# A hybrid vision network on one core: the depthwise stages' tile transfers, rings and share of blocks on TensorE

## The chip, the core and the metric

The program runs on one core of a Trainium2 chip. The core has TensorE (PE, matrix products into PSUM), VectorE (DVE), ScalarE (ACT), GpSimd (POOL) and SyncE (SP, which here issues nearly all DMAs), and sixteen DMA engines that move data between HBM and the on-chip memory (SBUF). Each engine runs its own instructions in order and waits on semaphores for the others. A wait on SP therefore holds up every transfer behind it. The metric is the device time of one execution in microseconds.

## The reference

The network takes 32 images of 96 channels and 32 x 32 pixels, float32, through four layers. What matters here is the second half of layer 0, an MLP over four volumes of eight frames, with a depthwise 3 x 3 x 3 convolution before each of its two channel products:

```python
def dsconv3d(x, dw_w, dw_b, pw_w, pw_b):
    y = jax.lax.conv_general_dilated(x, dw_w, (1, 1, 1), [(1, 1)] * 3,
                                     dimension_numbers=('NCDHW', 'OIDHW', 'NCDHW'), feature_group_count=x.shape[1])
    y = jax.nn.gelu(y + dw_b[None, :, None, None, None], approximate=False)
    y = jnp.einsum('bcdhw,oc->bodhw', y, pw_w) + pw_b[None, :, None, None, None]
    return y

def mlp(x, t, h, w, p):
    ...
    xg = dsconv3d(xg, p['dw1_w'], p['dw1_b'], p['pw1_w'], p['pw1_b'])   # 96 channels, then 96 -> 384
    xg = dsconv3d(xg, p['dw2_w'], p['dw2_b'], p['pw2_w'], p['pw2_b'])   # 384 channels, then 384 -> 96
```

So dw1 convolves 96 channels and dw2 384, each over 4 volumes x 8 frames of 1024 pixels, with 27 taps for each channel, zero beyond the edges, and a bias and GELU behind. The rest of the network (selective scans, convolutions, Fourier mixing, a quantised feed-forward) is untouched by the change.

## The kernel before

The kernel is one program of stages, each a function with its own SBUF and PSUM tensors; a stage begins when the one before has ended. `build` calls `volume_conv` for dw1 (line 2986), `l0_expand` (the product 96 to 384, stage `pw`), `volume_conv` for dw2 (line 2989), then `l1_in_proj`. In the profile both depthwise stages carry the tile prefix `dw_`.

`volume_conv` (line 936) takes the channels in blocks of 32. Of each three blocks two go through TensorE and one through taps, side by side. Three blocks are a *step*; a block on TensorE is a *unit*. dw1 has 1 step (2 units), dw2 has 4 steps (8 units).

**TensorE's way.** A tile holds 4 frames x 32 channels on 128 partitions and 1024 pixels, 512 KB. SP loads it (`load_raw`, line 1014; two buffers), DVE transposes it in 32 x 32 squares (`turn_in`, line 1216) into `xin`, where a partition is a frame and a column x, and the free dimensions are channel and row y. Eight tiles fill a unit. For each of the 32 channels PE multiplies banded matrices (`wb`, three rows of taps) and small edge matrices for the frames next to the group of four (`we`): 3 whole and 6 edge products in the code, each run as two matmuls in the trace. Weights for two channels (a pair) come by three DMAs (`load_weights`, line 1020) into four slots; a slot is loaded again when PE is done with the pair four before. ACT adds the bias, applies GELU and writes into `stg` (`evacuate`, line 1131); PSUM holds 8 channels. When a unit's 32 channels are there, DVE transposes its eight tiles back (`turn_back`, line 1225) into `ot` (three buffers), and SP stores them (`store_tile`, line 1035). `stg` holds one unit, so ACT's first evacuation of a unit waits for all eight back transposes of the unit before (line 1134).

**The taps' way.** For the third block a partition is a volume and a channel. The eight frames lie in `vol`, one buffer each (`load_frame`, line 1029). For each frame DVE does 15 taps (10 for the first and last frame) by multiply-and-add in PSUM (`pd`), ACT opens `acc` with one tap and makes 11 products (7) that POOL adds into `acc`; DVE merges both sums into `sm`, ACT adds bias and GELU in `close`, SP stores (`store_frame`, line 1041).

**Order.** Each engine's order is written out by hand. DVE runs all eight back transposes of a unit in one go at the start of the next (line 1248), and one transpose in after each six taps (line 1271). ACT spreads evacuations among its products by a count of operations (`catch_up`, line 1170), none before the ninth. SP's list goes by unit and pair j (line 1061): weights three pairs ahead, two tile stores at each j below 4, raw loads and frames at fixed j. The first loads of a stage are lines 1046 to 1060.

A tile moves by one DMA whose DRAM side has the shape (4, 32, 1024), 4 frames or 4 volumes by 32 channels.

Of the kernel before, what the change touches and what calls it, by code (L numbers as in the profile page):

```python
# [935 lines left out]
def volume_conv(nc, stage, src, dst, band, edge, bias, taps_w, steps, func):  # L936

    T = 8
    PAIRS, SLOTS = 16, 4
    PRODS, RAWS, OUTS = 4, 2, 3  # L940
    UNITS = 2 * steps
# [36 lines left out]
    def block_of(u):  # L978
        return 3 * (u // 2) + u % 2

    def four_frames(of, u, t):
# [4 lines left out]
    def all_volumes(of, i, f):  # L986
        block = 3 * i + 2
        return of.rearrange("(v f) c n -> f v c n", f=FRAMES)[f, :, 32 * block:32 * block + 32, :]

    with ExitStack() as stack:  # L990
        r = Room(nc, stage, stack)
        xin = r.sb("xin", [128, 2, 32, T, SIDE])
        stg = r.sb("stg", [128, 32, T, SIDE])
        raw = r.sb("raw", [128, RAWS, HW]); ot = r.sb("ot", [128, OUTS, HW])
        wb = r.sb("wb", [128, SLOTS, 2, 3, 128]); we = r.sb("we", [128, SLOTS, 2, 2, 3, 32])
        vol = r.sb("vol", [128, FRAMES, HW])
# [4 lines left out]
        s_raw = [r.dma_sem(f"raw{k}") for k in range(RAWS)]  # L1001
        s_band = [r.dma_sem(f"band{k}") for k in range(SLOTS)]
        s_vol = [r.dma_sem(f"vol{f}") for f in range(FRAMES)]
# [6 lines left out]

        with nc.Block() as block:
            @block.sync
            def _(sp):
                def load_raw(q):
                    if q < T * UNITS:
                        if q >= RAWS:
                            sp.wait_ge(turned, nth(q - RAWS))
                        sp.dma_start(raw[:, q % RAWS, :], four_frames(src, q // T, q % T)).then_inc(s_raw[q % RAWS], 16)

                def load_weights(q):  # L1020
                    if q < PAIRS * UNITS:
                        k = q % SLOTS
                        if q >= SLOTS:
                            sp.wait_ge(mm, nth(2 * (q - SLOTS) + 1))
                        sp.dma_start(wb[:, k, :, :, :], band[q]).then_inc(s_band[k], 16)
                        sp.dma_start(we[0:32, k, 0, :, :, :], edge[q, 0]).then_inc(s_band[k], 16)
                        sp.dma_start(we[96:128, k, 1, :, :, :], edge[q, 1]).then_inc(s_band[k], 16)

                def load_frame(i, f):
                    if i < steps:  # L1030
                        if i > 0:
                            sp.wait_ge(merged, nth((i - 1) * FRAMES + min(f + 1, FRAMES - 1)))
                        sp.dma_start(vol[:, f, :], all_volumes(src, i, f)).then_inc(s_vol[f], 16)

                def store_tile(u, t):
                    if u >= 0:
                        q = T * u + t
                        sp.wait_ge(back, nth(q))
                        sp.dma_start(four_frames(dst, u, t), ot[:, q % OUTS, :]).then_inc(s_ot[q % OUTS], 16)

                def store_frame(i, f):
                    if i >= 0:
                        sp.wait_ge(done, nth(i * FRAMES + f))
                        sp.dma_start(all_volumes(dst, i, f), sm[:, f % 2, :]).then_inc(s_sm[f % 2], 16)
# [6 lines left out]
                for f in range(3):  # L1051
                    load_frame(0, f)
                    load_raw(2 + 2 * f)
                    load_raw(3 + 2 * f)
                load_weights(1)
                load_weights(2)
                for f in range(3, FRAMES):
                    load_frame(0, f)
                load_raw(8)
                load_raw(9)  # L1060
                for u in range(UNITS):
                    i, s = u // 2, u % 2
                    for j in range(PAIRS):
                        load_weights(PAIRS * u + j + 3)
                        if j < 4:
                            store_tile(u - 1, 2 * j)
                            store_tile(u - 1, 2 * j + 1)
                        if j == 4 and s == 0:
                            load_frame(i, 5) if i else None
                            load_frame(i, 6) if i else None  # L1070
                            load_frame(i, 7) if i else None
                        if j == 4 and s == 1:
                            load_frame(i + 1, 1)
                            load_frame(i + 1, 2)
                        if j in (4, 6, 8, 9, 11, 13, 14, 15):
                            load_raw(T * (u + 1) + (4, 6, 8, 9, 11, 13, 14, 15).index(j) + RAWS)
                        if j == 5:
                            store_frame(i if s else i - 1, 2 if s else 6)
                            store_frame(i if s else i - 1, 3 if s else 7)
                        if j == 10 and s == 0:  # L1080
                            load_frame(i + 1, 0)
                        if j == 10 and s == 1:
                            load_frame(i + 1, 3)
                            load_frame(i + 1, 4)
                        if j == 13:
                            store_frame(i, 4 * s)
                            store_frame(i, 4 * s + 1)
# [2073 lines left out]
```

## Time and profile before

| | us |
|---|---|
| median of 3 runs | 19247.6 (19228.68 to 19251.41) |
| profiled execution | 19248.37 |
| its span | 19246.6, mean TensorE clock 0.947 |
| PE, DVE, ACT, POOL busy over the span | 88%, 85%, 80%, 67% |
| first transfer of dw1 to first of `pw` | 6046.46 to 6400.70 |
| first transfer of dw2 to first of the next stage | 6598.58 to 7820.44 |

The page gives busy time for the whole span; the two depthwise stages are 8% of it, so their limits show only in stretches cut out of it. PE's clock is shown as a share of its full speed; the two levels are 1.2 and 2.4 GHz, 0.50 and 1.00. In timelines the instructions of one kind that follow each other are merged: "x6" and the length of all six. The DMA share is the mean busy share of the sixteen DMA engines.

### The profile page before, as it was taken

Reading aid. Unit: us, or ns where it says so; the run is one execution under the profiler, and the core shown is the slowest. Engines: PE = TensorE matmul, PEld = TensorE weight load, DVE = VectorE, ACT = ScalarE, POOL = GpSimd, SP = SyncE. Lnnn points to the kernel's source line nnn. Section 1 sums busy time; section 2 is a strip of 40 time slices with the busy share of each in tenths; the row PEclk is TensorE's granted clock in tenths of the full one; section 3 lists DMA queues with packets and bytes.
Section 4 is the critical chain, followed back from the end, with each engine's and each line's share of the span. In section 5 each row is a group of like instructions: output and inputs, shape, how many; then the busy total and the mean of one; then the engine's idle time right before and its main releaser. Section 6 shows DMA issues by size and latency. Waiting matters only on the chain. (4 is left out here: it accounts for less than half of the span.)

```text
span 19246.6 us, 270014 instructions
## 1 busy us (share of the span) xinstructions
PE 16951.7 (88%) x77576; PEld 10108.8 (53%) x77576; DVE 16299.4 (85%) x12434; ACT 15364.9 (80%) x24406; POOL 12882.4 (67%) x6390
## 2 busy tenths in 40 slices
PE   8799997899985565798899999999999999989798
PEld 3455553555542244344466666666666666547374
DVE  4799998899975276378899999999999999979798
ACT  7699996899962444476699999999999999835556
POOL 0199991799952265154499999999999999800101
PEclk9899998999987787899999999999999999999899
DMA  5788876787886543656633333333333333352313
GB/s 176 233 241 242 247 242 211 236 243 236 251 228 187 194 139 135 223 214 257 266 112 111 111 112 117 112 111 118 116 111 112 117 112 111 111 160 57 103 52 98
DMA packets 857608, 3157.91 MB, mean 164 GB/s; under 512 B 106166, under 2 KB 139674, under 8 KB 831644
## 3 DMA queue, kind: packets, MB, share of 16 engines
q1 hardware_dynamic: 842396, 3091.03, 50.0%
q10 hardware_dynamic: 13824, 50.34, 0.7%
q8 instruction: 631, 10.34, 0.2%
q14 instruction: 757, 6.20, 0.1%
HBM read 2335.65 MB, written 805.32 MB: 163 GB/s over the span
## 5 line engine op out<-in xcount | busy, mean ns | idle before, releaser
L1929 DVE TENSOR_TENSOR_SCAN l1s_h<-l1s_da,l1s_pd 128x1024 f32<-128x1024 f32 x3072 | 6783.1, 2268 | 236.9 <-PE l1s_pd L1861 161.4
L1972 ACT ACTIVATE l1s_dm<-l1s_dut,l1s_bt 128x384 f32<-128x384 f32 x7424 | 4061.7, 605 | 74.8 <-PE l1s_pd L1861 74.6
L1955 ACT ACTIVATE l1s_da<-l1s_dl,l1s_a 128x1024 f32<-128x1024 f32 x3072 | 3502.0, 1140 | 30.7 <-DVE l1s_h L1929 29.6
L1861 PE MATMUL l1s_pd<-l1s_id,l1s_dm 128*128 128x128 f32 x22272 | 2973.0, 275 | 36.3 <-DVE l1s_h L1929 33.9
L1861 PEld LDWEIGHTS l1s_pd<-l1s_id,l1s_dm 128*128 128x128 f32 x22272 | 2562.1, 142 | 492.0 <-issue 288.2
L1835 POOL TENSOR_TENSOR l1s_pb<-l1s_h,l1s_cc 128x1024 f32<-128x1024 f32 x1024 | 2519.5, 2460 | 86.1 <-DVE l1s_h L1929 75.6
L1839 POOL TENSOR_TENSOR l1s_pa<-l1s_sm,l1s_cc 128x1024 f32<-128x1024 f32 x1024 | 2435.2, 2378 | 0.0
L1872 PE MATMUL l1s_py<-l1s_pb,l1s_both 128*128 128x512 f32 x4096 | 2157.2, 608 | 193.7 <-POOL l1s_pb L1835 193.5
L1830 POOL TENSOR_TENSOR l1s_sm<-l1s_h 128x1024 f32<-128x1024 f32 x928 | 2204.7, 2376 | 130.2 <-DVE l1s_h L1929 130.1
L1872 PE MATMUL l1s_py<-l1s_pa,l1s_id 128*128 128x512 f32 x4096 | 2114.4, 598 | 0.3 <-POOL l1s_pa L1839 0.3
L2795 POOL TENSOR_TENSOR l0sf_pr<-l0sf_h,l0sf_cc 128x1024 f32<-128x1024 f32 x768 | 1811.5, 2375 | 67.5 <-DVE l0sf_h L2877 52.7
L2795 POOL TENSOR_TENSOR l0sb_pr<-l0sb_h,l0sb_cc 128x1024 f32<-128x1024 f32 x768 | 1812.6, 2377 | 61.7 <-DVE l0sb_h L2877 57.5
L2540 POOL CAST ffn_h<-ffn_z 128x1024 fp8e5<-128x1024 f16 x128 | 180.9, 1414 | 2260.1 <-DVE ffn_z L2560 2237.6
L1855 PEld LDWEIGHTS l1s_pd<-l1s_bd,l1s_dut 128*128 128x128 f32 x4608 | 832.6, 191 | 1463.7 <-issue 825.5
L2833 PE MATMUL l0sf_py<-l0sf_pr,l0sf_id 128*128 128x512 f32 x3072 | 1580.0, 597 | 0.0
L2833 PE MATMUL l0sb_py<-l0sb_pr,l0sb_id 128*128 128x512 f32 x3072 | 1578.9, 596 | 0.0
L2925 ACT ACTIVATE l0sb_dm<-l0sb_dut,l0sb_bt 128x192 f32<-128x192 f32 x3584 | 1316.4, 447 | 9.2 <-DMA l0sb_dl<-l0dlsb 9.2
L2925 ACT ACTIVATE l0sf_dm<-l0sf_dut,l0sf_bt 128x192 f32<-128x192 f32 x3584 | 1313.6, 443 | 9.6 <-DMA l0sf_dl<-l0dlsf 9.6
L1210 POOL TENSOR_TENSOR dw_acc<-dw_acc,dw_prod 128x961 f32<-128x961 f32 (+2 forms) x400 | 897.0, 2288 | 552.8 <-ACT dw_prod L1158 550.3
L2813 PEld LDWEIGHTS l0sf_pd<-l0sf_id,l0sf_dm 128*128 128x128 f32 x6144 | 762.4, 142 | 928.1 <-issue 683.8
L2813 PEld LDWEIGHTS l0sb_pd<-l0sb_id,l0sb_dm 128*128 128x128 f32 x6144 | 761.9, 142 | 922.9 <-issue 680.8
L1112 PE MATMUL dw_pc<-dw_xin,dw_wb 128*128 128x248 f32 (+1 forms) x1920 | 572.2, 433 | 615.7 <-DMA dw_we<-in_dw_edge 222.6
(310 smaller groups left out, 31634.3 us busy)
## 6 DMA issues: line engine op xcount, KB each, us to landing
l1s_cc<-crows SPq DMA_DIRECT2D x1024, 512.0 KB, 3.7
l0sf_cc<-l0crowsf SPq DMA_DIRECT2D x512, 512.0 KB, 5.4
l0sb_cc<-l0crowsb SPq DMA_DIRECT2D x512, 512.0 KB, 5.4
l0sf_cc<-l0crowsf SPq DMA_DIRECT2D x512, 256.0 KB, 7.1
l0sb_cc<-l0crowsb SPq DMA_DIRECT2D x512, 256.0 KB, 7.0
dls<-l1p_dl SPq DMA_DIRECT2D x192, 512.0 KB, 6.9
duts<-l1p_dut SPq DMA_DIRECT2D x64, 1536.0 KB, 5.9
l1s_dut<-duts SPq DMA_DIRECT2D x64, 1536.0 KB, 7.2
```

The source lines that it names most:

```text
L1830: pool.tensor_tensor(sm[:, rnd % 2, :], h[:, rnd * HT % 4, :], h[:, (rnd * HT + 1) % 4, :], ALU.add)\
L1835: pool.tensor_tensor(pb[:, rnd % 2, :], h[:, (rnd * HT + 2) % 4, :], cc[:, rnd % 4, :], ALU.mult)\
L1839: pool.tensor_tensor(pa[:, rnd % 2, :], sm[:, rnd % 2, :], cc[:, rnd % 4, :], ALU.mult)\
L1861: mm = pe.transpose(pd[:, s % 2, blk * 128:blk * 128 + 128], dm[:, rnd % 2, blk, j * 128:j * 128 + 128], idt[:, :])
L1872: mm = pe.matmul(target[:, hs], weights[:, :], row[:, hs], start=(rnd == 0), stop=(rnd == ROUNDS - 1))
L1929: dve.tensor_tensor_scan(h[:, s % 4, :], da[:, j, :], pd[:, s % 2, :], 0.0, ALU.mult, ALU.add)\
L1955: act.activation(da[:, j, :], dl[:, half, j, :], ACT.Exp, scale=a[:, HT * half + j, n:n + 1])\
L1972: ins = act.activation(dm[:, rnd % 2, blk, :], dut[:, half, blk, :], ACT.Identity, scale=bt[:, half, blk, n:n + 1])
L2795: pool.tensor_tensor(pr[:, s % 4, :], h[:, s % 6, :], cc[:, rnd % 4, j, :], ALU.mult).then_inc(prod, 1)
L2813: mm = pe.transpose(pd[:, half, at:at + 128], dm[:, rnd % 2, blk, COLUMNS[j]:COLUMNS[j] + 128], idt[:, :])
L2833: mm = pe.matmul(py[:, j, HALVES[half]], idt[:, :], pr[:, s % 4, HALVES[half]], start=(n == 0), stop=(n == N - 1))
L2925: ins = act.activation(out, src, ACT.Identity, scale=b)
```

## The change

- `volume_conv` takes `per_step`, the blocks on TensorE per step. dw1 keeps 2 (of 3). dw2 gets 3 of 4: 3 steps, 9 units and 3 tap blocks in place of 4 steps, 8 units and 4 tap blocks.
- Each tile and each frame moves by four DMAs of 32 rows (128 KB) in place of one. Semaphores count 64 a tile.
- One more tap of the six inner frames goes from DVE to ACT and POOL (12 products in place of 11).
- `stg` becomes a ring of 48 channels in three halves of 16. The middle unit of three starts with its second 16 channels (`in_order`). ACT waits for back transposes two units old before its first half and one unit old before its second.
- `vol` becomes a ring of 6 frames, weights have 3 slots (from 4), products 3 (from 4), `ot` 2 buffers (from 3). At the start of a stage tiles 2 to 5 land in `ot` and `sm`.
- DVE's transposes in and back are placed among the taps by their share of the unit. ACT's evacuations are spread over the step, with no minimum of nine. SP's order is by slice of a step.
- The tables on the host are laid out for the new blocks.

```diff
-    PAIRS, SLOTS = 16, 4
-    PRODS, RAWS, OUTS = 4, 2, 3
-    UNITS = 2 * steps
+    PAIRS, SLOTS = 16, 3
+    PRODS, RAWS, OUTS, RING = 3, 2, 2, 6
+    UNITS = per_step * steps
...
-        share = 11 if len(depths) == 3 else 7
+        share = 12 if len(depths) == 3 else 7
...
+    def four_frames(u, t):
 
         first = t % SEQS * FRAMES + t // SEQS * 4
-        return of[first:first + 4, 32 * block_of(u):32 * block_of(u) + 32, :]
+        rows = channels((per_step + 1) * (u // per_step) + u % per_step)
+        return [(slice(32 * j, 32 * j + 32), first + j, rows) for j in range(4)]
...
+    def in_order(u, n):
+        return (n + 16) % 32 if u % 3 == 1 else n
...
                 def load_raw(q):
                     if q < T * UNITS:
-                        if q >= RAWS:
-                            sp.wait_ge(turned, nth(q - RAWS))
-                        sp.dma_start(raw[:, q % RAWS, :], four_frames(src, q // T, q % T)).then_inc(s_raw[q % RAWS], 16)
+                        to, sem, _ = landing(q)
+                        if q >= 6:
+                            sp.wait_ge(turned, nth(q - 6 if q < 8 else q - RAWS))
+                        for rows, image, of in four_frames(q // T, q % T):
+                            sp.dma_start(to[rows, :], src[image, of, :]).then_inc(sem, 16)
...
                 load_raw(0)
                 load_raw(1)
                 load_all(sp, s_w, consts)
+                for f in range(3):
+                    load_frame(0, f)
+                for q in range(2, 6):
+                    load_raw(q)
                 sp.wait_ge(zeroed, nth(0))
                 load_weights(0)
...
                 load_weights(1)
+                load_raw(6)
+                load_raw(7)
+                for f in range(3, RING):
                     load_frame(0, f)
                 load_raw(8)
...
+                for i in range(steps):
+                    for j in range(SLICES):
+                        u, w = per_step * i + j // PAIRS, j % PAIRS
+                        load_weights(PAIRS * u + w + 2)
+                        if w % 2 == 0:
+                            load_raw(T * (u + 1) + w // 2 + 1)
+                        if 2 <= w < 10:
+                            store_tile(u - 1, w - 2)
+                        if j == at(0.04) and i:
+                            load_frame(i, 3)
+                            load_frame(i, 4)
+                            load_frame(i, 5)
+                        if j == at(0.15):
+                            store_frame(i - 1, 6)
+                            store_frame(i - 1, 7)
+                        if j == at(0.27):
+                            load_frame(i, 6)
+                        if j == at(0.40):
+                            store_frame(i, 0)
+                            store_frame(i, 1)
...
-                    if c == 0 and u:
+                    if n == 0 and u > 1:
+                        act.wait_ge(back, nth(T * (u - 1) - 1))
+                    if n == 16 and u:
                         act.wait_ge(back, nth(T * u - 1))
                     act.wait_ge(mm, nth(q | 1))
...
-                        while out < 32 and max(9, (out // 2 + 1) * steps_here // 16 + 1) <= passed:
-                            evacuate(u, out)
+                        while out < CHANNELS * (i + 1) and (out % CHANNELS // 2 + 1) * WHOLE // (CHANNELS // 2) + 1 <= passed:
+                            evacuate(out)
...
+                        share = (n + 1) * per_step / TAPS + per_step * i
+                        while outs < T * UNITS and share >= outs // T + 1 + 0.06 + 0.06 * (outs % T):
+                            turn_back(outs)
+                            outs += 1
+                        while share >= ins // T - 1 + (ins % T + 1) / T and ins < T * UNITS:
+                            turn_in(ins)
+                            ins += 1
...
-                w["dw2_band"], w["dw2_edge"], w["dw2_bias"], w["dw2_taps"], 4, ACT.Gelu)
+                w["dw2_band"], w["dw2_edge"], w["dw2_bias"], w["dw2_taps"], 3, 3, ACT.Gelu)
```

## Rows read from the trace of the kernel before

**Rows 1.** Stretches: length; busy (count) PE, PEld, DVE, ACT, POOL; clock; DMA share; GB/s

```profile
6046.46:6400.70 354.24, 153.82 (x1152) 109.65 (x1152) 196.10 (x150) 127.30 (x161) 180.68 (x81) 0.71 0.33 112
6598.58:7820.44 1221.86, 669.92 (x4608) 458.33 (x4608) 782.26 (x600) 496.33 (x640) 719.04 (x321) 0.76 0.38 130
6598.58:6663.87 65.29, 0.00 (x0) 0.00 (x0) 15.16 (x9) 9.53 (x9) 11.35 (x6) 0.50 0.32 113
6925.29:7502.00 576.71, 341.89 (x2303) 230.94 (x2302) 390.84 (x301) 246.66 (x320) 359.30 (x161) 0.79 0.40 137
7759.89:7820.44 60.55, 0.00 (x0) 0.00 (x0) 14.95 (x9) 1.26 (x2) 0.00 (x0) 0.50 0.22 87
6066.50:6095.50 29.00, 0.00 (x0) 0.00 (x0) 7.61 (x4) 1.15 (x1) 0.00 (x0) 0.50 0.26 105
6162.00:6198.00 36.00, 36.00 (x291) 26.36 (x291) 29.50 (x24) 27.73 (x36) 35.69 (x17) 1.00 0.55 159
6410.00:6580.00 170.00, 165.01 (x358) 61.12 (x357) 0.00 (x0) 98.53 (x90) 0.00 (x0) 0.99 0.96 337
```

**Rows 2.** Timeline, dw1's lead-in, DVE: start, length, instruction, [idle before <- releaser]

```profile
6056.54 1.90 DVE L1222 STREAM_TRANSPOSE dw_xin<-dw_raw 128x1024 f32<-128x1024 f32 x1 [16.27 <-DMA dw_raw<-n]
6061.54 1.90 DVE L1222 STREAM_TRANSPOSE dw_xin<-dw_raw 128x1024 f32<-128x1024 f32 x1 [3.09 <-DMA dw_raw<-n]
```

**Rows 3.** Waits in dw2: us in total, times, longest

```profile
DVE dw_xin L1222 <- DMA dw_raw<-hid: 432.1, 27, 232.5
...
ACT dw_stg L1136 <- DVE dw_ot L1232: 289.9, 7, 44.1
...
DVE dw_ot L1232 <- DMA g<-dw_ot: 191.0, 40, 11.5
```

**Rows 4.** Timeline, SP's DMA issues in dw1

```profile
6133.06 1.05 SPq L1026 DMA_DIRECT2D dw_we<-in_dw_edge  x1
...
6157.98 0.35 SPq L1025 DMA_DIRECT2D dw_wb<-in_dw_band  x1
6158.37 0.43 SPq L1026 DMA_DIRECT2D dw_we<-in_dw_edge  x1
6158.84 0.42 SPq L1027 DMA_DIRECT2D dw_we<-in_dw_edge  x1
...
6162.44 0.35 SPq L1025 DMA_DIRECT2D dw_wb<-in_dw_band  x1
```

**Rows 5.** DMA issues between dw1 and dw2: count, KB each, median us to landing

```profile
hid<-pw_out ACTq DMA_DIRECT2D x96, 512.0 KB, 3.9
...
pw_wt<-in_pw SPq DMA_DIRECT2D x1, 144.0 KB, 2.1
```

**Rows 6.** Timeline, PE in dw1, DVE and POOL in dw2

```profile
6150.80 1.22 PE L1112 MATMUL dw_pc<-dw_xin,dw_wb 128*128 128x256 f32 x2 [24.19 <-DMA dw_we<-in_dw_edge]
...
6744.75 6.93 DVE L1262 SCALAR_TENSOR_TENSOR dw_pd<-dw_vol,dw_wt,dw_pd 128x992 f32<-128x992 f32 x6
6751.60 1.99 DVE L1222 STREAM_TRANSPOSE dw_xin<-dw_raw 128x1024 f32<-128x1024 f32 x1
...
6712.96 81.11 POOL L1210 TENSOR_TENSOR dw_acc<-dw_acc,dw_prod 128x992 f32<-128x992 f32 x36 [24.69 <-ACT dw_prod L1158]
```

**Rows 7.** Groups of dw2 by form: busy us, mean ns, idle before

```profile
L1158 ACT ACTIVATE dw_prod<-dw_vol,dw_wt 128x961 f32<-128x961 f32 x176 | 188.1, 1100 | 48.3 <-POOL dw_acc L1210 48.1
...
L1222 DVE STREAM_TRANSPOSE dw_xin<-dw_raw 128x1024 f32<-128x1024 f32 x64 | 125.8, 1965 | 432.1 <-DMA dw_raw<-hid 432.1
L1232 DVE STREAM_TRANSPOSE dw_ot<-dw_stg 128x1024 f32<-128x1024 f32 x64 | 120.9, 1908 | 191.0 <-DMA g<-dw_ot 191.0
...
L1136 ACT ACTIVATE dw_stg<-dw_pc,dw_bt 128x256 f32<-128x256 f32 x256 | 106.7, 476 | 525.4 <-DVE dw_ot L1232 289.9 <-PE dw_pc L1112 235.4
...
L1240 DVE TENSOR_TENSOR dw_sm<-dw_pd,dw_acc 128x1024 f32<-128x1024 f32 x32 | 37.6, 1214 | 11.1 <-POOL dw_acc L1210 10.1 <-issue 0.9
```

More of the change, by code:

```diff
@@ L1001, in volume_conv @@
         s_raw = [r.dma_sem(f"raw{k}") for k in range(RAWS)]
+        s_lead = [r.dma_sem(f"lead{k}") for k in range(4)]
         s_band = [r.dma_sem(f"band{k}") for k in range(SLOTS)]
-        s_vol = [r.dma_sem(f"vol{f}") for f in range(FRAMES)]
+        s_vol = [r.dma_sem(f"vol{k}") for k in range(RING)]
         s_ot = [r.dma_sem(f"ot{k}") for k in range(OUTS)]
@@ L1058, in _ @@
+                load_raw(7)
+                for f in range(3, RING):
                     load_frame(0, f)
                 load_raw(8)
[L1060 to L1072, printed above, removed]
+                SLICES = PAIRS * per_step
@@ L1082, in _ @@
[L1082 to L1087, printed above, removed]
+                        if j == at(0.92):
+                            store_frame(i, 4)
+                            store_frame(i, 5)
                 for t in range(T):
@@ L1092, in _ @@
                 for k in range(OUTS):
-                    sp.wait_ge(s_ot[k], 16 * len(range(k, T * UNITS, OUTS)))
+                    sp.wait_ge(s_ot[k], 64 * T * UNITS // OUTS)
                 for k in range(2):
-                    sp.wait_ge(s_sm[k], 16 * steps * FRAMES // 2)
+                    sp.wait_ge(s_sm[k], 64 * steps * FRAMES // 2)
             @block.tensor
@@ L1270, in _ @@
                             merge(i, f + 1)
-                        if (n - start) % 6 == 5 and turned_in < T:
-                            turn_in(u + 1, turned_in)
-                            turned_in += 1
-                for t in range(T):
-                    turn_back(UNITS - 1, t)
+                        share = (n + 1) * per_step / TAPS + per_step * i
[5 more added lines that the diff above has]
+                            ins += 1
+                while outs < T * UNITS:
+                    turn_back(outs)
+                    outs += 1
 def l0_expand(nc, g1, w, hid):
@@ L3085, in volume_tables @@
                 rows[z][:, :, :, to + x - 1, to] = cubes[:, :, z, :, x, None]
-        rows = rows.transpose(0, 1, 2, 4, 3, 5).reshape(3, steps * 16 * 2, 2, 32, 3, 32).swapaxes(2, 3)
-        band = np.zeros((steps * 32, 4, 32, 2, 3, 4, 32), f)
+        pairs = steps * per_step * 16
+        rows = rows.transpose(0, 1, 2, 4, 3, 5).reshape(3, pairs, 2, 32, 3, 32).swapaxes(2, 3)
+        band = np.zeros((pairs, 4, 32, 2, 3, 4, 32), f)
         for to in range(4):
@@ L3090, in volume_tables @@
                 band[:, of, :, :, :, to] = rows[of - to + 1]
-        flat = blocks[:, 2].repeat(4, axis=0).reshape(steps, 4, 32, 27).reshape(steps, 128, 27)
-        parts = offsets.reshape(steps, 3, 32)
-        last = parts[:, 2].repeat(4, axis=0).reshape(steps, 128, 1)
-        return {"band": band.reshape(steps * 32, 128, 2, 3, 128), "edge": np.stack([rows[2], rows[0]], 1),
-                "bias": np.broadcast_to(parts[:, :2].reshape(1, steps * 2, 32), (128, steps * 2, 32)),
-                "taps": cat([flat, last], 2).swapaxes(0, 1)}
-    for name in ("dw1", "dw2"):
-        for part, table in volume_tables(v[f"L0_conv_{name}_w"], v[f"L0_conv_{name}_b"]).items():
+        parts = offsets.reshape(steps, per_step + 1, 32)
+        last = cat([blocks[:, per_step], parts[:, per_step, :, None]], 2)
+        bias = parts[:, :per_step].reshape(1, steps * per_step, 32)
+        return {"band": band.reshape(pairs, 128, 2, 3, 128), "edge": np.stack([rows[2], rows[0]], 1),
+                "bias": np.broadcast_to(bias, (128, steps * per_step, 32)),
+                "taps": last[:, None].repeat(4, axis=1).reshape(steps, 128, 28).swapaxes(0, 1)}
+    for name, per_step in (("dw1", 2), ("dw2", 3)):
+        for part, table in volume_tables(v[f"L0_conv_{name}_w"], v[f"L0_conv_{name}_b"], per_step).items():
             w[f"{name}_{part}"] = table
```

183 lines of the change are left out of this document (98 added, 85 removed).

## The prediction

> **What bounds the kernel now.** I read the page first: its 40 slices show one stretch, near a third of the span, where every engine is partly idle, and its groups place the depthwise program there. A chain of waits for the last instruction is of no use here, since that ends in another stage. So I cut the span by the first transfer of each stage [rows 1]: dw1 lasts 354.2 us and dw2 1221.9 us, of which 65.3 us pass before its first tap and 60.6 us after its last merge. In the two middle steps (576.7 us, 288.4 us each) PE is busy 59%, DVE 68%, ACT 43%, POOL 62%, and the 16 DMA engines 40% at 137 GB/s. No engine is the bound.
>
> The transfers are. Two tiles of 512 KB, issued together, release their transposes at 6056.54 and 6061.54 [rows 2]: 5.0 us a tile. In a stretch that moves only such tiles the DMA share is 0.26 at 105 GB/s, while the stage between dw1 and dw2 moves 337 GB/s at 0.96 [rows 1]. So a tile transfer runs at the pace of about four engines of sixteen. A step of dw2 moves 48 tiles (16 loads and 16 stores of transposed tiles, 8 and 8 frames): 48 x 5.0 = 240 us. Its 32 pairs of weights (432 KB a pair, over all engines) take of each engine a sixteenth of 432 KB, at 512/4 KB in 5.0 us: 1.05 us, 34 us a step. Together 274 of 288 us: the four engines are full. The waits agree: transposes back wait 191 us for stores, transposes in 432 us for loads (232.5 us of it between the stages) [rows 3].
>
> The Trainium skill says why, in "DMA: Bandwidth & Descriptors", section "Why a DMA increments its semaphore by 16 and not by 1": a transfer is spread over the largest number up to 16 that divides the slowest dimension of both sides. A source of (4, 32, 1024) gets 4, and the trace agrees (0.26 of 16 is 4.2). For 32 rows it gives 16. No row of before shows a 128 KB transfer of 32 rows, so the new width stays a bet, which I carry as a rival.
>
> **Part 1, four DMAs of 32 rows.** I take it that they use all engines: the transfers of the stage that reaches 0.96 have 96 or 128 rows in a single dimension, the tiles have 4 by 32, and the pieces again a single one. So the 5.0 us go; one 512 KB piece of work then takes 512 KB / 337 GB/s = 1.6 us [rows 1]. What is late next is SP, which issues them. Back-to-back issues start 0.47 us apart, the 32-row edge loads among them [rows 4]; behind full queues the same instruction took 1.05 us [rows 4]. A tile costs SP 4 x 0.47 = 1.88 us, a pair of weights 3 issues, 1.3 us. A new step of dw2 has 48 x 3 + 48 x 4 + 16 x 4 = 400 issues, 188 us (before: 144). Bytes: 64 tiles and 48 pairs are 54 MB, in 250 us 217 GB/s, below 337.
>
> The lead-in: SP issues two tiles, 2 constants, three frames, four tiles, 6 weight pieces and two tiles, 52 issues; the last starts after 51 x 0.47 = 24.0 us, lands some 2.3 us later, and its transpose of 1.9 us [rows 7] ends at 28.4 us with 0.2 us to wake DVE. The landing is my choice between 2.1 us for 144 KB and 3.9 us for 512 KB at full load [rows 5]. Against 65.3 us this saves 37 us in each stage.
>
> The tail: with two buffers each store (1.88 us and landing) holds the next transpose but one, 5.6 us for two. Eight end 20.6 us after the merge, then one tile and two frames are issued (5.6 us) and land: 28 us, and 2 to 3 us to the next stage. Before: 60.6 us.
>
> **Part 2, three of four blocks on TensorE in dw2.** Nine units instead of eight, three steps of taps instead of four. PE at full clock takes 4.46 us for two channels, seen in the distance of the weight issues that wait for it [rows 4], with PE busy 36.00 of 36.00 us at clock 1.00 [rows 1]: 71.4 us a unit. DVE has 104 taps a step (110 less the one tap moved for each of six inner frames), at 1.14 us from start to start, and 48 transposes at 1.85 us [rows 6], and 8 merges [rows 7] at 1.14 us: 118.6 + 88.8 + 9.1 = 216.5 us, 72.2 us a unit. POOL has 86 adds at 81.11/36 = 2.25 us [rows 6]: 194 us. ACT has 96 evacuations of 0.48 us and 86 products and 16 whole frames of 1.1 us each [rows 7]: 158 us. PE and DVE are level, and POOL is hidden under both in dw2.
>
> **Part 3, the order on SP and two buffers.** This is where I put a new wait. In slice w of a unit (one slice per channel pair) SP loads weights; in even slices it then waits for a transpose in and issues a raw tile; in slices 2 to 9 it then stores a tile back. DVE's back transpose t+2 waits until store t has landed, because OUTS is 2. So from one transpose in to the next, over two slices: raw 1.88 us, store 3 x 0.47 us to its last piece, landing 2.3 us; then on DVE back, two taps, back, transpose in, 8.0 us. Sum 13.6 us, against 8.9 us that PE needs for two slices. The loop turns three times: the first transpose in ends at 5 taps and three transposes, 11.3 us, the fourth at 52.1 us; the rest of the unit is 16.7 taps, four transposes and its merges, 29.4 us. A unit lasts 81.5 us instead of 72. Behind SP in this loop stand the weights, so PE stalls too. After a wait PE's first pair is slow: started at 6150.80 [rows 6], done by 6157.98 [rows 4], 7.2 us instead of 4.46. I add 3 us a unit for one such pair and for the 64 frame issues a step: 84.5 us. Bounds of a unit: 72.5 us if landing and order hide everything, 91 us with landing 3.9 us and issue 0.56 us.
>
> The end of a step is a loop of its own: last product, add, merges, transpose in, PE's next unit, some 5.7 us, twice. The first unit has no backs (71.4 + 2.7), the last no loads (76).
>
> The longer stage queue costs nothing in bandwidth; SLOTS 3 instead of 4 gives weights two pairs, 8.9 us, for 1.3 us of issue and the landing, enough unless SP is late, which is in the 3 us. PRODS 3 instead of 4: POOL ran 36 adds without a gap with ACT at 1.1 us beside its 2.25 us, so nothing. The ring of six frames: frame 7 waits for merge 2 and is read a quarter of a step later; nothing. The ring of 48 channels takes away ACT's wait for all eight back transposes (289.9 us) [rows 3]; PE's stalls behind it go with that.
>
> **Sum, dw2:** 28.4 + 74.1 + 7 x 84.5 + 76 + 2 x 5.7 + merges and tail 35 = 816 us, against 1221.9: 406 us saved.
>
> **dw1** has one step, two units, no raw loads in the second, so the loop does not turn: stores come at PE's pace. POOL bounds it. ACT now evacuates the first pair before its fourth product, so POOL's fourth add starts when PE's first pair is done: 28.4 + 7.2 + 1.9 = 37.5 us. Then 83 adds x 2.25 = 187 us, 5 us where ACT waits for unit 1 to begin, merges 2.3, tail 28, 2 us over: 262 us, against 354.2: 92 us saved.
>
> The profiled execution took 19248.4 us, its span 19246.6, the median of runs 19247.6, so they may be used for one another. 19248 - 406 - 92 = 18750 us. Under 0.2% of the total (39 us) a measurement can't tell a change from none.
>
> **Rivals.**
> (a) The loop is hidden; the stage runs at PE's and DVE's 73 us a unit: 28 + 74 + 8 x 73 + 11 + 35 = 733 us. 18,667 us. For it: DVE's waits for stores come in a bunch today and are spread by the change. Against it: two buffers, and SP in order. 0.16.
> (b) SP is dearer than 0.47 us an issue, for the queues are partly filled: at 0.8 us a step needs 320 us of SP, a unit 107 us, dw2 970 us, dw1 20 us more: 18,920 us. For it: 1.05 us in a burst [rows 4]. Against it: those bursts stood behind four-engine tiles, which go. 0.13.
> (c) The change doesn't do what it says: 32-row pieces move at 105 GB/s too. dw2 moves 3 x 64 tiles, the same 192 as before: 3 x (320 + 50) + 95 = 1205 us, dw1 as before. 19,230 us. 0.04.
> (d) Slower: each issue holds SP's queue for longer than 0.94 us on average. dw2 has 1200 issues, and 1200 x 0.94 + 95 us is the 1222 us of today; that is the point from which it decides. At 1.1 us: 1415 us, and dw1 near 354: 19,440 us. Such an issue (1.05 us) is in the trace only behind full queues; in the steady row it is 0.47. 0.04.
>
> The Trainium skill, in "DMA: Bandwidth & Descriptors", speaks for (d) in the section "Anatomy of one DMA — SWDGE (gpsimd) path": a fixed 2.0 us beside bytes at 436 GB/s. By its figures a 128 KB piece is 2.3 us, four in series 9.2 us, 192 tiles 1770 us. The trace contradicts the series: 96 stores and 32 loads of a mean 480 KB keep 337 GB/s with 3.9 us to landing each [rows 1, 5], so transfers overlap and the fixed part is a delay.
>
> **Chances.** Forecast 0.63, between 18,700 and 18,850 on its own bounds. The low end of the range is (a), 18,665; the high end 18,850 is the loop at 91 us a unit with slower tails (7 x 6.5 = 46 us, and as much again for SP's lateness). Faster by over 0.2%: forecast, (a), (b) and a part of the rest, 0.94; within 0.2%: most of (c), 0.03; slower 0.03.
>
> **What would show it.** DMA share against GB/s in dw1's first 30 us: 279 GB/s or so instead of 105 at 0.26. dw2's stage length 816 us, first PE matmul 28 us after the first issue. DVE's back transposes waiting for stores in the middle units, some 12 us a unit; if they wait for nothing, (a). The issues on SP 0.47 us apart; if more, (b) or (d). In dw1 POOL without gaps after 38 us. I am wrong in mechanism if units of 84 us come with DVE waiting for evacuations or merges and not for stores.

## The result, and the profile after

The kernel after takes 18782.0 us (median of 4 runs, 18774.3 to 18805.6), the kernel before 19238.1 us in the same comparison: ratio 0.9769, 95% interval 0.9755 to 0.9782. Forecast: 18750 us, range 18665 to 18850.

The stretches of the profiled execution after: dw1, dw2, its lead-in, its middle step, its tail. The columns are those of [rows 1]:

```profile
6031.70:6297.20 265.50, 153.26 (x1152) 109.05 (x1152) 189.22 (x144) 135.12 (x167) 193.94 (x87) 0.78 0.55 149
6495.40:7359.30 863.90, 694.26 (x5184) 491.98 (x5184) 654.84 (x480) 428.58 (x594) 582.42 (x259) 0.90 0.68 192
6495.40:6527.26 31.86, 0.01 (x1) 0.01 (x1) 15.30 (x9) 3.31 (x3) 3.37 (x2) 0.50 1.00 241
6786.40:7068.50 282.10, 233.45 (x1728) 164.74 (x1728) 217.96 (x161) 144.25 (x200) 196.17 (x87) 0.92 0.69 196
7325.10:7359.30 34.20, 0.00 (x0) 0.00 (x0) 17.00 (x10) 2.28 (x2) 0.00 (x0) 0.54 0.55 154
```

dw1 takes 265.5 us (before 354.2), dw2 863.9 us (before 1221.9): 446.7 us less. The two executions differ by 20 us more outside these stages, in code that the change leaves alone. The start of dw1 alone lies between 6019 and 6047 us in the thirteen profiled executions of this study, so lengths of stages are compared below, and totals only to about 20 us. Stages whose code is the same repeat closely: dw1 took 265.5 and 264.7 us (after, two_of_three), 234.0 and 233.0 (pool_start_dw1, late_evacuations), 233.5 and 232.9 (both_orders, late_and_order).

The middle step of dw2 (282.1 us, the fourth row) carries 196 GB/s at a DMA share of 0.69, where [rows 1] had 137 at 0.40. PE is busy 83% of it, DVE 77%, POOL 70%. Who waits in dw2 (total, times, longest):

```profile
ACT dw_stg L1177 <- PE dw_pc L1151: 305.0, 121, 22.7
POOL dw_acc L1252 <- ACT dw_prod L1200: 244.9, 54, 22.2
...
DVE dw_ot L1275 <- DMA g<-dw_ot: 120.6, 28, 10.4
...
PE dw_pc L1151 <- DMA dw_we<-in_dw_edge: 92.1, 27, 8.7
ACT dw_stg L1177 <- DVE dw_ot L1275: 77.3, 8, 13.6
...
DVE dw_sm L1284 <- POOL dw_acc L1252: 35.7, 4, 10.9
```

Against [rows 3]: DVE's wait for stores went from 191.0 to 120.6 us, though a store now lands 2.8 us after its issue (columns: count, KB each, median us from issue to landing, in the middle step):

```profile
dw_wb<-in_dw_band SPq DMA_DIRECT2D x48, 384.0 KB, 3.3
dw_raw<-hid SPq DMA_DIRECT2D x96, 128.0 KB, 3.2
g<-dw_ot SPq DMA_DIRECT2D x96, 128.0 KB, 2.8
```

The wait predicted for two buffers is there in the form predicted. One turn of the loop in the middle step, DVE first, then SP:

```profile
6812.98 1.96 DVE L1265 STREAM_TRANSPOSE dw_xin<-dw_raw 128x1024 f32<-128x1024 f32 x1
6814.80 2.31 DVE L1304 SCALAR_TENSOR_TENSOR dw_pd<-dw_vol,dw_wt,dw_pd 128x961 f32<-128x961 f32 x2
6821.50 1.93 DVE L1275 STREAM_TRANSPOSE dw_ot<-dw_stg 128x1024 f32<-128x1024 f32 x1 [4.38 <-DMA g<-dw_ot]
6823.36 2.34 DVE L1304 SCALAR_TENSOR_TENSOR dw_pd<-dw_vol,dw_wt,dw_pd 128x961 f32<-128x961 f32 x2
6825.60 1.94 DVE L1275 STREAM_TRANSPOSE dw_ot<-dw_stg 128x1024 f32<-128x1024 f32 x1
6827.47 1.89 DVE L1265 STREAM_TRANSPOSE dw_xin<-dw_raw 128x1024 f32<-128x1024 f32 x1
```

```profile
6814.97 1.70 SPq L1041 DMA_DIRECT2D dw_raw<-hid  x4
6816.72 2.63 SPq L1067 DMA_DIRECT2D g<-dw_ot  x4
```

The transpose in ends at 6814.94, SP issues the raw tile at once, then the store; DVE's back transpose waits for this store and starts at 6821.50, 2.2 us after SP has issued its last piece; two taps, a back, the next transpose in. From in to in 14.5 us, where 13.6 was forecast. Part of the difference is the store's four issues, 2.63 us here instead of 1.88. This turn is among the shorter ones: the 21 turns of the seven units with both loads and stores take 13.6 to 20.7 us, 16.2 on average. In the middle step SP itself waits 44.0 us for transposes in and 32.9 us for PE.

### The profile page after: what moved, and what is told of

The parts are those of the page before. It is cut to its first block and busy times, and to the rows that moved or that the text cites. A ratio compares the mean times of both kernels' runs of the same rounds, so it can differ in the third digit from the quotient of the medians.

```text
span 18779.8 us, 271646 instructions
## 1 busy us (share of the span) xinstructions
PE 16964.4 (90%) x78152; PEld 10133.1 (54%) x78152; DVE 16165.3 (86%) x12308; ACT 15304.7 (81%) x24366; POOL 12759.8 (68%) x6334
## 5 line engine op out<-in xcount | busy, mean ns | idle before, releaser
L1902 PE MATMUL l1s_pd<-l1s_bd,l1s_dut 128*128 128x128 f32 x4608 | 946.3, 287 | 182.6 <-issue 71.2
L2918 DVE TENSOR_TENSOR_SCAN l0sf_h<-l0sf_da,l0sf_st,l0sf_pd 128x512 f32<-128x512 f32 x768 | 981.8, 1278 | 116.8 <-PE l0sf_pd L2860 41.3
```

Source lines behind the costliest of these rows:

```text
L1902: pe.matmul(pd[:, s % 2, LAST * 128:], dut[:, half, LAST, j * 128:j * 128 + 128], bd[:, DIAGONAL.index(n), :], start=True, stop=True)
```

## The experiments

Lengths in us from one profiled execution each; the time is the median of its runs, the ratio is to the kernel before with its 95% interval.

| kernel | dw1 | dw2 | time | ratio |
|---|---|---|---|---|
| before | 354.2 | 1221.9 | | |
| after | 265.5 | 863.9 | 18782.0 | 0.9769 (0.9755 to 0.9782) |
| one_dma_per_tile | 356.6 | 1363.3 | 19378.0 | 1.0077 (1.0057 to 1.0097) |
| before_four_dmas | 246.6 | 862.0 | 18751.3 | 0.9751 (0.9732 to 0.9771) |
| two_of_three | 264.7 | 950.9 | 18863.5 | 0.9810 (0.9790 to 0.9829) |
| three_out_buffers | 259.6 | 792.0 | 18715.4 | 0.9731 (0.9714 to 0.9747) |
| store_before_raw | 264.5 | 810.3 | 18735.3 | 0.9743 (0.9726 to 0.9759) |
| eight_pieces | 301.3 | 1082.7 | 19036.2 | 0.9901 (0.9881 to 0.9921) |
| one_weight_dma | 260.6 | 802.0 | 18724.3 | 0.9737 (0.9721 to 0.9754) |
| pool_start_dw1 | 234.0 | 792.4 | 18684.6 | 0.9721 (0.9705 to 0.9737) |
| late_evacuations | 233.0 | 775.6 | 18667.9 | 0.9708 (0.9691 to 0.9724) |
| both_orders | 233.5 | 775.6 | 18664.0 | 0.9709 (0.9693 to 0.9725) |
| late_and_order | 232.9 | 758.0 | 18636.1 | 0.9696 (0.9680 to 0.9713) |

**One DMA per tile again.** The one edit, at all four places where a tile or frame moves, with semaphore counts to match:

```diff
-                        for rows, image, of in four_frames(q // T, q % T):
-                            sp.dma_start(to[rows, :], src[image, of, :]).then_inc(sem, 16)
+                        sp.dma_start(to, whole_tile(src, q // T, q % T)).then_inc(sem, 16)
```

> The kernel after, with each tile and frame moved by one DMA of shape (4, 32, 1024) again, all else as after. Theory (tiles ran at the pace of four engines, and their width is what the change buys): a step of dw2 has 64 tiles at 5.0 us = 320 us and 48 pairs of weights at 1.05 us = 50 us on the same four engines, so three steps take 1110 us, and with lead-in 65 and tail 60 dw2 takes about 1200 to 1240 us, dw1 about 350 us; total 19200 or above, within 0.5% of the kernel before. Rival (the gain is in DVE's and ACT's new order and the block moved to TensorE): dw2 stays under 1000 us and the total under 18950.

```profile
6602.40:7965.70 1363.30, 772.66 (x5184) 528.70 (x5184) 656.32 (x480) 427.78 (x594) 581.69 (x259) 0.76 0.37 121
```

The whole gain is gone and dw2 is 141 us slower than before the change, 0.77% on the total. The theory stands, and its number is too low by over 120 us. The share of 0.37 is a mean over sixteen engines and hides that four of them are nearly full. By the packet records of this trace, the middle step (456.6 us) has 1446 us of 4096-byte packets, nearly all of them tiles, 362 on each of four engines, and 1218 us of weights and the rest, 76 on each of sixteen: some 438 of 457 us on the four. The forecast had 320 + 50 = 370. So a pair of weights costs each engine about 1.5 us and not the 1.05 us of the forecast and of the prediction, and a tile's packet takes 175 ns on average, where it took 159 ns in the stretch of [rows 1] with tiles alone. That tiles run on just four engines is the assumption in this estimate; the records don't name the engine.

**The kernel before with four DMAs.**

```diff
-                        sp.dma_start(raw[:, q % RAWS, :], four_frames(src, q // T, q % T)).then_inc(s_raw[q % RAWS], 16)
+                        for rows, image, of in four_frames(q // T, q % T):
+                            sp.dma_start(raw[rows, q % RAWS, :], src[image, of, :]).then_inc(s_raw[q % RAWS], 16)
```

> The kernel before with only the transfers changed: each tile and frame by four DMAs of 32 rows. Theory: the four-engine bound goes, and what is left is the order: all eight back transposes in one go, with ACT and PE waiting for them. DVE has 207 us a step of two units, and each unit adds some 15 us of waiting, so a unit takes 105 to 115 us against 144, dw2 about 930 to 990 us, dw1 about 275 us, total about 18880 to 18960. Rival (the order matters most and the transfers only fit it): dw2 over 1100 us. Rival (the transfers are everything): dw2 at 864 us or less, total at 18780.

```profile
6475.60:7337.60 862.00, 625.31 (x4608) 443.52 (x4608) 782.83 (x600) 502.85 (x640) 719.31 (x321) 0.83 0.64 184
```

```profile
ACT dw_prod L1164 <- POOL dw_acc L1216: 169.3, 188, 1.2
...
ACT dw_stg L1142 <- DVE dw_ot L1238: 115.8, 7, 17.7
...
DVE dw_ot L1238 <- DMA g<-dw_ot: 29.2, 21, 2.1
...
PE dw_pc L1118 <- DMA dw_we<-in_dw_edge: 12.5, 4, 4.1
```

The rival "the transfers are everything" holds: 862.0 us in dw2, and 246.6 in dw1, 19 us better than the whole change; the totals are too close for their intervals to tell apart. My theory had 930 to 990 us: I took 15 us of waiting a unit, with PE and ACT stopped behind the eight back transposes. The waits in the second fence are short, 115.8 us for ACT in seven units, 29.2 us for stores with three buffers, 12.5 us for weights, and yet a unit takes 102 us. The reason is DVE's own work. Four of the middle units (two steps):

```profile
6691.10:7099.90 408.80, 314.38 (x2304) 222.49 (x2304) 391.26 (x302) 251.26 (x321) 359.08 (x161) 0.85 0.67 193
```

DVE is busy 391.3 of 408.8 us, 96%, and PE 77%. With quick tiles the kernel before is bound by DVE, and moving a block from the taps to TensorE is what takes work off DVE. That only pays where nothing else holds a unit up, which the next runs show.

**Two of three blocks in dw2, within the kernel after.**

```diff
-                w["dw2_band"], w["dw2_edge"], w["dw2_bias"], w["dw2_taps"], 3, 3, ACT.Gelu)
+                w["dw2_band"], w["dw2_edge"], w["dw2_bias"], w["dw2_taps"], 4, 2, ACT.Gelu)
```

> The kernel after with dw2 at two of three blocks on TensorE and four steps, as before the change. Theory (the loop sets a unit's length): a unit has 52 taps, the loop ends at about 60 us, the rest is 42 us: 102 us a unit, 8 units, dw2 about 880 to 900 us; moving the third block to TensorE is worth 20 to 40 us only. Rival (POOL, 194 us a step, sets it): 97 us a unit, about 850 us. Rival (the split is a main part of the gain): dw2 over 950 us.

dw2 took 950.9 us, so the rival "a main part" is right at its edge and the theory 50 us short. With this kernel the change is taken apart, in dw2: transfers 1221.9 to 862.0 (-359.9); new order, rings, two out buffers in place of three and the one tap a frame 862.0 to 950.9 (+88.9); the third block on TensorE 950.9 to 863.9 (-87.0). The last two cancel. This holds for this order of the steps alone, and how the 88.9 us divide was not tried; three_out_buffers below takes 71.9 us off the kernel with the third block by the buffer alone. In dw1, which has no third block, the kernel after is 18.9 us behind before_four_dmas. The third buffer gives back 5.9 us of it (259.6). POOL's six more adds, 86 instead of 80 at 2.25 us, are 13.5 us by an estimate. So the order itself costs dw1 next to nothing.

**Three out buffers.**

```diff
-    PRODS, RAWS, OUTS, RING = 3, 2, 2, 6
+    PRODS, RAWS, OUTS, RING = 3, 2, 3, 6
```

> The kernel after with three buffers for tiles transposed back in place of two. Theory (loop of transpose in, raw issue, store issue, landing, back transpose): with three buffers a store gates the third back transpose behind it, the loop's 13.6 us for two slices fall to about 10.5 us, DVE's waits for stores (120.6 us in dw2) fall under 40 us, and a middle unit falls from 87 or more to 75 to 80 us: dw2 775 to 815 us, total 18700 to 18735. Rival (SP's 400 issues a step are the bound, by their number): dw2 stays within 15 us of 864, and waits move from stores to weights.

```profile
DVE dw_sm L1284 <- POOL dw_acc L1252: 42.8, 5, 13.2
ACT dw_stg L1177 <- DVE dw_ot L1275: 33.1, 8, 6.4
DVE dw_ot L1275 <- DMA g<-dw_ot: 32.4, 17, 4.5
```

72 us for 4 KB a partition. In the middle step SP's waits for transposes in fall from 44.0 to 17.6 us. Waits for stores fall to 32.4 us, ACT's for the ring from 77.3 to 33.1. Units 3 and 4 fall from 86.9 and 88.7 us (from the last transpose in of one unit to that of the next) to 76.2 and 78.9. Unit 5, the last of its step, falls only from 106.6 to 95.2.

**Store before raw load**, with two buffers:

```diff
-                        if w % 2 == 0:
-                            load_raw(T * (u + 1) + w // 2 + 1)
                         if 2 <= w < 10:
                             store_tile(u - 1, w - 2)
+                        if w % 2 == 0:
+                            load_raw(T * (u + 1) + w // 2 + 1)
```

> The kernel after (two out buffers) with two lines of SP's list exchanged: in each slice the store of a tile goes ahead of the raw load and of its wait for a transpose in. Same instructions, same number of issues. Theory (the loop through SP's wait is what lengthens a unit): the loop is then raw 1.88, weights 1.4, store 1.4 to its last piece, landing 2.3, back, transpose in, 10.7 us instead of 13.6 for two slices, three times in each of seven units: dw2 60 us shorter, 795 to 815 us, and DVE's waits for stores fall from 120 us to 40 to 70 us. Rival (only the number of buffers or of issues counts, not their order): dw2 within 15 us of 864.

```profile
DVE dw_ot L1275 <- DMA g<-dw_ot: 79.0, 30, 6.8
```

53.6 us less in dw2 from the place of one call, no instruction added or taken away. It is a second, independent cut through the loop, and waits fall less than forecast (79.0 us) but the stage as forecast. Number of issues alone is excluded as the cause.

**Eight pieces of 16 rows.**

```diff
-        return [(slice(32 * j, 32 * j + 32), first + j, rows) for j in range(4)]
+        return [(slice(16 * j, 16 * j + 16), first + j // 2, half(rows, j % 2)) for j in range(8)]
```

> The kernel after with each tile and frame by eight DMAs of 16 rows (64 KB) in place of four of 32. Bytes the same, the engines used the same by the theory of width. Theory (SP's issue time is close under the bound): 656 issues a step x 0.47 = 308 us, so three steps 925 us, lead-in about 45 us, tail about 50 us: dw2 1010 to 1060 us, dw1 290 to 310 us, total 18960 to 19030. Rival (issues are hidden, only landing and order count): dw2 under 900 us. Rival (a fixed cost of 2 us a transfer in series): over 1500 us.

```profile
6535.10:7617.80 1082.70, 731.71 (x5184) 507.15 (x5184) 656.46 (x480) 428.21 (x594) 582.27 (x259) 0.84 0.62 153
```

1082.7 us, 219 more, and dw1 301.3: twice the issues for each tile and frame, 656 in a step instead of 400, move the bound to SP. They take 308 us at 0.47; 1082.7 less lead-in and tail (some 95) is 329 a step. In the middle step (359.9 us) SP waits only 42.0 us for DVE and PE, where it waits 76.9 of 282.1 us in the kernel after, and the DMA engines aren't full at 0.62. The rival of transfers in series (over 1500 us) is excluded.

**One weight DMA**, with three out buffers. The two edge matrices become columns of the banded table, zero outside their rows:

```diff
                         sp.dma_start(wb[:, k, :, :, :], band[at]).then_inc(s_band[k], 16)
-                        sp.dma_start(we[0:32, k, 0, :, :, :], edge[at, 0]).then_inc(s_band[k], 16)
-                        sp.dma_start(we[96:128, k, 1, :, :, :], edge[at, 1]).then_inc(s_band[k], 16)
```

> As three_out_buffers, with banded and edge matrices of a pair in one table and one DMA of 576 KB instead of three of 432 KB: 304 issues a step instead of 400, a third more weight bytes. Theory (what is left over the floor is SP coming late to the weights): PE's waits for weights, 50.6 us there, fall under 20 us, the late end of each step shrinks with them, dw2 745 to 775 us against 792, total 18665 to 18700. Rival (bytes on the DMA engines are what delays weights; they were 73% busy): no gain or a loss, dw2 790 or more.

```profile
dw_wb<-in_dw_band SPq DMA_DIRECT2D x74, 576.0 KB, 5.8
g<-dw_ot SPq DMA_DIRECT2D x158, 128.0 KB, 4.2
```

No gain (802.0 against 792.0). With a quarter of the issues gone and a third more weight bytes, landing grew: weights 5.8 us, where three_out_buffers has 3.3, and stores 4.2, where it has 2.8. The DMA share rose from 0.73 to 0.79. PE's waits for weights stayed, 51.5 us against 50.6. That SP's issues are what is left was my theory, and it fell. Fewer issues and more bytes came together in this run, so what each did isn't shown apart.

**POOL's start and share in dw1**, with three out buffers:

```diff
-        share = 12 if len(depths) == 3 else 7
+        share = (12 if steps > 1 else 10) if len(depths) == 3 else 7
...
-                        while out < CHANNELS * (i + 1) and (out % CHANNELS // 2 + 1) * WHOLE // (CHANNELS // 2) + 1 <= passed:
+                        while out < CHANNELS * (i + 1) and max(0 if i else 9, (out % CHANNELS // 2 + 1) * WHOLE // (CHANNELS // 2) + 1) <= passed:
```

> As three_out_buffers, with two things of POOL's side: in the first step ACT makes no evacuation before its ninth operation (as before the change), and in dw1 alone DVE takes two taps a frame back (10 products in place of 12, 74 adds in place of 86). Theory (dw1 is bound by POOL from its start, and the early evacuation holds POOL up until PE's first pair is there): POOL's adds start near 14 us and run on, 74 x 2.25 = 167 us; DVE's 116 taps and transposes end at about 199 us; dw1 230 to 240 us against 259.6, dw2 within 8 us of 792. Rival (dw1 is bound by PE or the transposes): dw1 within 8 us of 259.6.

POOL's adds in dw1, first after, then in this kernel:

```profile
6047.61 4.57 POOL L1252 TENSOR_TENSOR dw_acc<-dw_acc,dw_prod 128x992 f32<-128x992 f32 x2 [14.85 <-ACT dw_prod L1200]
6072.37 101.22 POOL L1252 TENSOR_TENSOR dw_acc<-dw_acc,dw_prod 128x992 f32<-128x992 f32 x45 [20.20 <-ACT dw_prod L1200]
6177.50 87.80 POOL L1252 TENSOR_TENSOR dw_acc<-dw_acc,dw_prod 128x961 f32<-128x961 f32 x39 [3.91 <-ACT dw_prod L1200]
```

```profile
6062.43 15.74 POOL L1252 TENSOR_TENSOR dw_acc<-dw_acc,dw_prod 128x992 f32<-128x992 f32 x7 [14.87 <-ACT dw_prod L1200]
6096.61 74.27 POOL L1252 TENSOR_TENSOR dw_acc<-dw_acc,dw_prod 128x992 f32<-128x992 f32 x33 [18.44 <-ACT dw_prod L1200]
6177.54 76.44 POOL L1252 TENSOR_TENSOR dw_acc<-dw_acc,dw_prod 128x1024 f32<-128x1024 f32 x34 [6.66 <-ACT dw_prod L1200]
```

After, POOL makes two adds, waits 20.2 us for ACT, which stands before PE's first pair, and then runs almost without a gap for 193 us. Held back to the ninth operation, ACT lets seven adds through first. dw1 falls to 234.0 us, the forecast, but not for both reasons. The hold has moved, not gone: POOL waits 18.4 us behind its seventh add and 6.7 us later, 25.1 us in all, where it was 20.2 and 3.9, 24.1 us, and its first add comes 16 us into the stage in both. The gain, 25.6 us against three_out_buffers, is that of twelve fewer adds at 2.25 us, 27 us by an estimate. The later start of the evacuations gave nothing that these rows show.

**Late evacuations** at the end of a step. What they are aimed at, in the kernel after: ACT and then DVE at the end of the middle step.

```profile
7025.58 0.84 ACT L1177 ACTIVATE dw_stg<-dw_pc,dw_bt 128x256 f32<-128x256 f32 x2 [13.23 <-DVE dw_ot L1275]
...
7057.40 0.84 ACT L1177 ACTIVATE dw_stg<-dw_pc,dw_bt 128x256 f32<-128x256 f32 x2 [1.63 <-PE dw_pc L1151]
7058.13 2.08 ACT L1200 ACTIVATE dw_prod<-dw_vol,dw_wt 128x961 f32<-128x961 f32 x2
```

```profile
7048.57 5.05 DVE L1304 SCALAR_TENSOR_TENSOR dw_pd<-dw_vol,dw_wt,dw_pd 128x992 f32<-128x992 f32 x4
7064.33 2.36 DVE L1284 TENSOR_TENSOR dw_sm<-dw_pd,dw_acc 128x1024 f32<-128x1024 f32 x2 [10.71 <-POOL dw_acc L1252]
```

ACT waits 13.2 us for the last back transpose, because the ring's half is in use, and has evacuations behind it. PE's last pairs, also late for weights (waits of 8.7 and 3.7 us), hold ACT's last products. So POOL adds late, and DVE's merges start 10.7 us late. The edit, on pool_start_dw1:

```diff
+                        late = 6 if steps > 1 and pair >= 36 else 0
+                        return max(0 if i else 9, (pair + 1) * WHOLE // (CHANNELS // 2) + 1 + late)
```

> As pool_start_dw1 (three out buffers, dw1's POOL changes), and in dw2 ACT makes the evacuations of the last 12 pairs of each step six operations later. Theory (the long third unit of a step, 91 to 95 us against 76 to 82 for the others, comes from ACT waiting for PE's late pairs with the last products behind it, so that POOL's last adds and DVE's merges come late): POOL's last adds no longer wait for PE, DVE's waits for POOL before merges fall from 44 us to under 15, third units fall to about 82 us, dw2 765 to 775 us against 792. Rival (PE itself is late at a step's end for its weights, and the next unit can't begin before it ends anyway): third units stay over 88 us, dw2 within 8 us of 792.

Merges in pool_start_dw1 at the end of two steps, and the sum of such waits in dw2 with late evacuations:

```profile
7000.46 2.35 DVE L1284 TENSOR_TENSOR dw_sm<-dw_pd,dw_acc 128x1024 f32<-128x1024 f32 x2 [12.52 <-POOL dw_acc L1252]
...
7241.84 2.35 DVE L1284 TENSOR_TENSOR dw_sm<-dw_pd,dw_acc 128x1024 f32<-128x1024 f32 x2 [12.85 <-POOL dw_acc L1252]
```

```profile
DVE dw_sm L1289 <- POOL dw_acc L1257: 16.0, 3, 9.0
```

Third units fall from 91.0 and 94.2 to 84.4 and 85.7 us, the waits of merges from 44.1 to 16.0 us, dw2 by 16.8 us, a little less than the 17 to 27 forecast. The other units did not gain (79.0 to 81.2 us, where they took 77.3 to 80.9), and third units stay some 5 us longer than they are.

**Both orders and the fastest version.** The store ahead of the raw load, on pool_start_dw1 and on late_evacuations; same edit as above.

> As pool_start_dw1, with the store ahead of the raw load in each slice. Theory (with three buffers the store loop is already shorter than DVE's own work in two slices, 10.5 us, so the order has nothing left to give): dw2 782 to 798 us, within 10 us of 792. Rival (the two cuts add, 54 us here and 72 us there): dw2 about 740 us.

dw2 775.6 us: the order gives 16.8 us with three buffers where it gave 53.6 with two. The theory (nothing left) is 6 us off its band, the rival (they add) 36 us off. Mostly the same loop, then, but not all: DVE's waits for stores fall from 28.4 to 13.3 us, and PE's waits for weights, which stand behind the same calls on SP, from 47.7 to 33.0.

> As late_evacuations, with the store ahead of the raw load. Theory: as late_evacuations within 8 us in dw2, 762 to 780 us, total 18655 to 18680, the fastest of all. Rival (SP is late at the step's end and the order shifts it): over 785 us.

```profile
6448.30:7206.30 758.00, 661.63 (x5184) 474.37 (x5184) 655.87 (x480) 431.41 (x594) 582.04 (x259) 0.94 0.77 218
```

758.0 us, PE busy 87% of the stage at clock 0.94. The total, 18636.1 us, is the fastest of all: its four runs (18625.8 to 18659.1) lie under all runs of the others. It has a ratio of 0.9696 to the kernel before, 0.75% under that of the kernel after. Its middle step:

```profile
6710.80:6948.10 237.30, 222.80 (x1737) 159.08 (x1737) 218.27 (x161) 143.91 (x200) 193.78 (x86) 0.97 0.82 233
```

PE is busy 94% and DVE 92% of it, 79.1 us a unit, and SP waits 2.2 us for transposes in. The loop is out of the way here, and the two engines that were to be level are.

## Why the prediction was right, and what in it was off

**What bounds the kernel before: shown.** Four-engine tiles were the bound. The sum for it, 240 us of tiles and 34 of weights in a step of 288 us, is too low in its terms: the packet records of the two middle steps give 256 us a step of 4096-byte packets on each of four engines and 49 us of weights on each of sixteen. That is over 288 us, so it can't be exact, but full either way. With whole tiles again the kernel after loses everything; four pieces alone bring the kernel before all of it. The first 30 us of dw1, in the kernel after:

```profile
6031.70:6061.70 30.00, 0.00 (x0) 0.00 (x0) 13.75 (x8) 5.60 (x5) 5.62 (x3) 0.50 0.99 235
```

They moved 235 GB/s at a share of 0.99, where 279 were forecast and [rows 1] had 105 at 0.26: the pieces do use all sixteen engines. The rule of the Trainium skill that gave this ("DMA: Bandwidth & Descriptors", section "Why a DMA increments its semaphore by 16 and not by 1") agrees with both shares. A row of the Trainium skill's "DMA: Bandwidth & Descriptors", section "Rules for kernel authors", advises one 128-partition transfer in place of two to disjoint halves, since both halves use all sixteen engines anyway. These tiles lack that premise, and the runs decide for dividing them: 1221.9 us with one transfer, 862.0 with four.

**Part 1: right.** The pieces use all engines. PE's first matmul comes 31.9 us after the first issue, 28.4 forecast, 65.5 before. The last raw tile's issues end 24 us in, as forecast; its pieces land 5.9 us behind their issue (median) and not 2.3, with the DMA engines full. The tail is 34.2 us with two merges, 35 forecast; without them it is 31.9 us, where it was 60.6.

**Part 2: right in the sum, hidden in the measure.** PE and DVE were to be level at 72 us a unit. No unit with back transposes reached that in the kernel after; the first, which has none, took 69.8 us by the transposes in. The third block is worth 87 us, as much as the order and the rings with two out buffers had cost. The sum of part 2 is borne out by late_and_order, where PE and DVE are busy 74.3 and 72.8 us a unit (71.4 and 72.2 in the forecast) and a unit takes 79.1 us.

**Part 3: the mechanism right, the size nearly.** A turn of the loop was foreseen at 13.6 us and takes 16.2 on average. Units of 84.5 us were forecast, and the ones inside a step took 85.9 to 90.8. What I did not see is that this part, with its two out buffers, made the change no better than its first part alone, as I never worked out the kernel before with quick tiles, which DVE bounds at 102 us a unit.

**The mis-sized terms** are the loop's turn and the end of a step. Over 21 turns the loop took 55 us more than 13.6 us each. Most of this was made up in the rest of the units, also because the 3 us a unit that I had added are counted in it. What is left shows at the ends of steps, which I had at 5.7 us on top of a unit. Units 2 and 5 took 101.5 and 106.5 us, so 17 and 22 over 84.5, and 28 us over the forecast with its 5.7: 28 of the 48 us by which dw2 missed 816. The five other units with loads and stores add 18 us, the lead-in 3 and the last unit with the tail 3; the first unit took 4 less. A term that I put at nothing without a reason was the ring of 48 channels ("takes away ACT's wait"). The wait did not go: it is 77.3 us in dw2 at the ring's second half, where it was 289.9, behind the same loop. With three out buffers, late_evacuations shows that the order of ACT's evacuations at the step's end costs 7 to 9 us of each such unit.

**dw1: right**, 262 forecast and 265.5 measured, with POOL as the bound: its third add starts 40.7 us into the stage (the fourth at 37.5 in the forecast), and it then runs almost without a gap. pool_start_dw1 gains by giving POOL fewer adds; the early hold only moves in it.

**Rivals.** (a) failed in the kernel after; its 733 us is approached only by late_and_order (758.0). (b) was a part of the truth: the four issues of a store took 2.0 us on average in dw2, and up to 3.7. (c) and (d) are excluded by the middle step's 196 GB/s and by eight_pieces. The total was 32 us over the forecast: 51 us from the two stages, and 20 us back from the rest of the program, which the change leaves alone. That the total came so near is in part this luck.

## What to carry to other kernels

When no engine is the bound and the DMA share stays flat, compare GB/s with the share in a stretch with one kind of transfer: a share of four sixteenths at 105 GB/s is a transfer that is too narrow, and its shape is the first thing to change, alone, before any order is rewritten. A queue that waits for one engine before it issues what another waits for is a loop: count its turns, and try a third buffer or the exchange of two calls before a larger change. Several parts measured together can hide that two of them cancel. Before work is moved off an engine, look whether that engine is the bound once the transfers are quick: here DVE was, at 96%, and even so the kernel with the block moved to TensorE came under the 862.0 us of before_four_dmas only where SP's loop was shortened too (810.3, 792.0, 758.0).

## What was not expected of the hardware

Pieces of 128 KB fill the DMA engines earlier than their bytes say: in dw2's lead-in the share is 1.00 at 241 GB/s, where 384 and 512 KB transfers with one row dimension had 337 GB/s at 0.96 [rows 1]. With pieces of 64 KB dw2 runs at a share of 0.62 with 153 GB/s. So my 337 GB/s as the room above 217 was too generous. one_weight_dma, at 0.79 with 233 GB/s, may have run into this.

The packet records of the traces show where it comes from. Tiles move in packets of 4096 bytes in every kernel, and such a packet takes longer in the narrower pieces. On average it takes 159 ns for the whole tiles alone, 185 ns in the stage with 337 GB/s, 227 ns in the middle step of dw2 for pieces of 32 rows (271 ns in its lead-in), and 285 ns in that of eight_pieces for pieces of 16 rows. The reason is open; for the first two the number of engines at work at once differs too.
